# Expert stage of an attention and mixture-of-experts block: half-precision splitting in pairs of chunks, the second pair one tile later, and the routing weights applied on GpSimd

## What is computed

```python
a = xf @ W1a_e + b1a_e
b = xf @ W1b_e + b1b_e
y = jax.nn.silu(a) * b @ W2_e + b2_e
return (acc + w_e[:, None] * y, None)
```

## Time and profile before

| what | us |
|---|---|
| median of 3 runs | 671.4 (671.26 to 672.26) |
| span of the profiled execution, first to last instruction | 669.5 |
| from the first matmul of tile 2 to that of the last tile, 36 tiles | 160.99 |
| PE busy over the span | 575.0 |
| ACT busy, expert tiles 2 to 37 | 142.42 |
| DVE busy, the same tiles | 123.34 |

### The profile page before, as it was taken

One profiled execution on the slowest core, in us unless ns is written; L12 is line 12 of the kernel. 1 busy time (PEld: TensorE's weight loads), 2 busy tenths in 40 slices (PEclk: granted clock), 3 DMA queues, 4 the chain that ended last, 5 costly groups with the idle time before them and its releaser, 6 DMA issues.

```text
span 669.5 us, 19952 instructions
## 1 busy us (share of the span) xinstructions
PE 575.0 (86%) x5529; PEld 419.3 (63%) x5530; DVE 464.9 (69%) x1571; ACT 428.4 (64%) x1108; POOL 342.2 (51%) x501
## 2 busy tenths in 40 slices
PE   3599999999999999999999998218999999999700
PEld 1366666666666666666666665107888888888600
DVE  5665677787778768768767663454777777777646
ACT  3457665766767757766667655116888888888700
POOL 5432254565665655656656444650545545555553
PEclk9989999999999999999999999657999999999955
DMA  8212011112112112101212102132121211111066
GB/s 240 60 56 57 10 48 41 40 54 68 32 52 63 48 35 59 55 30 57 55 34 55 47 19 62 50 97 59 55 61 50 61 56 49 55 54 52 27 181 196
DMA packets 53668, 41.53 MB, mean 62 GB/s; under 512 B 7554, under 2 KB 48341, under 8 KB 53616
## 3 DMA queue, kind: packets, MB, share of 16 engines
q1 hardware_dynamic: 43056, 29.12, 16.4%
q0 software_dynamic: 4544, 8.54, 3.6%
q10 hardware_dynamic: 6016, 3.24, 1.6%
HBM read 24.80 MB, written 12.78 MB: 56 GB/s over the span
## 4 chain that ended last, share of the span: by engine, by line
PE 80%; DVE 7%; DMA 4%; issue 3%; ACT 2%; POOL 2%; SPq 0%; DVEq 0%; ACTq 0%; POOLq 0%
PE bank L1162 15%; PE bank L1126 8%; PE bank L1163 6%; PE bank L1319 5%; PE bank L1321 5%; PE bank L1320 5%; PE bank L1150 4%; PE bank L1139 4%; PE bank L1138 3%; PE bank L1340 3%; PE bank L1341 3%; PE bank L1114 3%; PE bank L1342 2%; PE bank L1175 2%; PE bank L1151 2%
## 5 line engine op out<-in xcount | busy, mean ns | idle before, releaser
L796 DVE TENSOR_REDUCE nmax<-bank 128x3 f32<-128x384 f32 x256 | 140.6, 555 | 75.5 <-PE bank L1126 71.1
L601 ACT ACTIVATE probs<-bank 128x384 f32<-128x384 f32 x256 | 126.7, 495 | 45.2 <-PE bank L1126 42.5
L1126 PE MATMUL bank<-cb,c 128*128 128x256 bf16 x512 | 140.6, 275 | 0.0
L554 POOL DMA_INDIRECT expert_outs<-y_sb,number_of x78 | 78.7, 1010 | 92.7 <-ACT y_sb L704 78.7
L1162 PE MATMUL bank<-probs,v_aug 128*32 128x256 f32 x512 | 119.1, 391 | 0.0
L1036 DVE SCALAR_TENSOR_TENSOR h<-bank,b_sb,silu_a 128x256 f32<-128x256 f32 x156 | 71.6, 479 | 51.4 <-ACT silu_a L715 51.2
L1319 PE MATMUL bank<-xt,we_hi 128*128 128x256 f16 x312 | 86.3, 277 | 1.9 <-ACT xt L689 0.8
L1320 PE MATMUL bank<-xt,we_hi 128*128 128x256 f16 x312 | 86.1, 276 | 0.0
L1321 PE MATMUL bank<-xt,we_lo 128*128 128x256 f16 x312 | 86.1, 276 | 0.0
L695 ACT ACTIVATE hh<-h 128x256 f16<-128x256 f32 x156 | 64.2, 411 | 19.1 <-DVE h L1036 14.4
L468 POOL DMA_INDIRECT expert_rows<-send,pos_i x64 | 63.3, 990 | 25.3 <-issue 12.2
(11 more groups left out here) (179 smaller groups left out, 1354.5 us busy)
## 6 DMA issues: line engine op xcount, KB each, us to landing
g_in<-expert_rows SPq DMA_DIRECT2D x39, 132.0 KB
k_pad<-qk_t SPq DMA_DIRECT2D x128, 32.0 KB, 1.9
mod_b<-mod_rows SPq DMA_DIRECT2D x16, 256.0 KB, 3.2
we_lo<-expert_outs SPq DMA_DIRECT2D x16, 256.0 KB, 3.9
wstage<-in_L_ffn_W1a_dram SPq DMA_DIRECT2D x16, 128.0 KB, 2.2
wstage<-in_L_ffn_W1b_dram SPq DMA_DIRECT2D x16, 128.0 KB, 2.3
wstage<-in_L_ffn_W_dram SPq DMA_DIRECT2D x16, 128.0 KB, 2.4
out_dram<-we_lo ACTq DMA_DIRECT2D x16, 128.0 KB, 3.5
```

Of the source, the lines that this page charges most:

```text
L554: pool.indirect_dma_start(out=outs, out_offset=bass.IndirectOffsetOnAxis(ap=number_of[:, r, s:s + 1], axis=0), in_=y_sb[:, r, s, :], in_of ...
L601: nc.scalar.activation(probs[:, k % 4], col_bank[k % 2][:, 0:S + P], ACT.Exp, scale=SM_SCALE).then_inc(probs_ready, 1)
L796: nc.vector.tensor_reduce(nmax[:, k], row_bank[k % 2][:, 0:3 * P].rearrange("p (c t) -> p c t", t=P), AX.X, ALU.max, negate=True).then_inc ...
L1126: return mm(diagonal, ident16, mask.unsqueeze(1).broadcast_to([P, 2, P]), start=False, stop=True, skip_group_check=True)
```

## The change

The copies `hh` and remainders `hl` are made for two chunks at once (512 columns) in place of one (256). The first pair (chunks 0 and 1) of tile j is made in tile j; the second pair (chunks 2 and 3) of tile j is made in tile j+1: on ACT behind the silu of chunk 0, on DVE behind h of chunk 1. `hl` counts two steps per tile in place of four. `weigh` leaves ACT: POOL multiplies by the weights (`tensor_scalar`, two instructions of 128 columns) ahead of its scatter. PE's list stays as it is.

```diff
@@ GpSimd, scatter(j) @@
-                pool.wait_ge(act_y, times(j, NS, NS))
+                pool.wait_ge(vec_y, times(j, 1, 1))
+                pool.wait_ge(named.sem, named.after(j, "weight"))
+                if due(times((j[0], 0, 1), 32)):
+                    pool.wait_ge(y_sent[r], times((j[0], 0, 1), 32))
                 pool.nop(nofuse=True)
                 for s in range(NS):
+                    nc.gpsimd.tensor_scalar(y_sb[:, r, s], yb[:, r % 2, s], weight_of[:, r, s:s + 1], 1.0, ALU.mult, ALU.mult).then_inc(pool_y, 1)
+                for s in range(NS):
+                    pool.wait_ge(pool_y, times(j, NS, s + 1))
+                    pool.nop(nofuse=True)
                     pool.indirect_dma_start(out=outs, ...
@@ ScalarE @@
-            def high(j, f):
-                act.wait_ge(vec_h, times(j, FB, f + 1))
+            def high(j, half):
+                two = slice(2 * half, 2 * half + 2)
+                act.wait_ge(vec_h, times(j, FB, 2 * half + 2))
                 if due(times(plus(j, -2), 1, 1)):
                     act.wait_ge(pe_y, times(plus(j, -2), 1, 1))
-                nc.scalar.activation(hh[:, j[1] % 2, f], h32[:, f], ACT.Copy).then_inc(act_hh, 1)
-
-            def weigh(j):
...
+                nc.scalar.activation(hh[:, j[1] % 2, two], h32[:, two], ACT.Copy).then_inc(act_hh, 1)
@@ ScalarE, tile(j), in the loop over f @@
-                    if f == 2 and finished:
-                        weigh(plus(j, -2))
+                    if f == 0 and following:
+                        high(plus(j, -1), 1)
                     if f == 2:
+                        high(j, 0)
                         read_next_experts(j)
-                    if f:
-                        high(j, f - 1)
-                high(j, FB - 1)
@@ VectorE @@
-            def low(j, f):
-                vec.wait_ge(act_hh, times(j, FB, f + 1))
-                nc.vector.tensor_tensor(hl[:, j[1] % 2, f], h32[:, f], hh[:, j[1] % 2, f], ALU.subtract).then_inc(vec_hl, 1)
+            def low(j, half):
+                two = slice(2 * half, 2 * half + 2)
+                vec.wait_ge(act_hh, times(j, 2, half + 1))
+                nc.vector.tensor_tensor(hl[:, j[1] % 2, two], h32[:, two], hh[:, j[1] % 2, two], ALU.subtract).then_inc(vec_hl, 1)
@@ VectorE, tile(j) @@
-                    if due(times(plus(j, -1), FB, f + 1)):
-                        vec.wait_ge(vec_hl, times(plus(j, -1), FB, f + 1))
+                    if due(times(plus(j, -1), 2, f // 2 + 1)):
+                        vec.wait_ge(vec_hl, times(plus(j, -1), 2, f // 2 + 1))
                     nc.vector.scalar_tensor_tensor(out=h32[:, f], ...
-                    if f >= 2:
-                        low(j, f - 2)
+                    if f == 1 and following:
+                        low(plus(j, -1), 1)
                     if f == 2:
                         read_next_experts(j)
-                low(j, FB - 2)
-                low(j, FB - 1)
+                low(j, 0)
@@ TensorE, project_out(j) @@
-                pe.wait_ge(vec_hl, times(j, FB, FB))
+                pe.wait_ge(vec_hl, times(j, 2, 2))
```

More of the change, by code:

```diff
@@ L269, in build @@
         pe_ab, act_silu, vec_h, act_hh, vec_hl = sem("pe_ab"), sem("act_silu"), sem("vec_h"), sem("act_hh"), sem("vec_hl")
-        pe_y, vec_y, act_y = sem("pe_y"), sem("vec_y"), sem("act_y")
+        pe_y, vec_y, pool_y = sem("pe_y"), sem("vec_y"), sem("pool_y")
         y_sent = [sem(f"y_sent{r}") for r in range(4)]
@@ L689, in save_x, with tile @@
                 nc.scalar.activation(xt[:, j[1] % 2], (chain_a16, chain_b16)[j[1] % 2][:, 0:2 * TS].rearrange("p (h t) -> p h t", t=TS), ACT.Copy).then_inc(act_x, 1)
-            def high(j, f):
-                act.wait_ge(vec_h, times(j, FB, f + 1))
+            def high(j, half):
+                two = slice(2 * half, 2 * half + 2)
+                act.wait_ge(vec_h, times(j, FB, 2 * half + 2))
                 if due(times(plus(j, -2), 1, 1)):
                     act.wait_ge(pe_y, times(plus(j, -2), 1, 1))
-                nc.scalar.activation(hh[:, j[1] % 2, f], h32[:, f], ACT.Copy).then_inc(act_hh, 1)
-            def weigh(j):
[L698 to L704, removed]
+                nc.scalar.activation(hh[:, j[1] % 2, two], h32[:, two], ACT.Copy).then_inc(act_hh, 1)
             known_experts, read_next_experts = experts_of(act)
-            def tile(j, more=True, finished=True):
+            def tile(j, more=True, following=True):
                 e = known_experts(j)[0]
@@ L717, in tile @@
                         save_x(plus(j, 1))
-                    if f == 2 and finished:
-                        weigh(plus(j, -2))
+                    if f == 0 and following:
+                        high(plus(j, -1), 1)
                     if f == 2:
+                        high(j, 0)
                         read_next_experts(j)
-                    if f:
-                        high(j, f - 1)
-                high(j, FB - 1)
             save_x(tile_number(0))
-            tile(tile_number(0), finished=False)
-            tile(tile_number(1), finished=False)
-            in_fours(act, 2, NT - 1, tile)
+            tile(tile_number(0), following=False)
+            in_fours(act, 1, NT - 1, tile)
             tile(tile_number(NT - 1), more=False)
-            weigh(tile_number(NT - 2))
-            weigh(tile_number(NT - 1))
+            high(tile_number(NT - 1), 1)
             out_v = out.rearrange("b (s p) d -> b p s d", p=P)
@@ L1019, in _, with tile @@
             vec.wait_ge(table, TABLE_STEPS)
-            def low(j, f):
-                vec.wait_ge(act_hh, times(j, FB, f + 1))
-                nc.vector.tensor_tensor(hl[:, j[1] % 2, f], h32[:, f], hh[:, j[1] % 2, f], ALU.subtract).then_inc(vec_hl, 1)
+            def low(j, half):
+                two = slice(2 * half, 2 * half + 2)
+                vec.wait_ge(act_hh, times(j, 2, half + 1))
+                nc.vector.tensor_tensor(hl[:, j[1] % 2, two], h32[:, two], hh[:, j[1] % 2, two], ALU.subtract).then_inc(vec_hl, 1)
             known_experts, read_next_experts = experts_of(vec)
-            def tile(j, finished=True):
+            def tile(j, finished=True, following=True):
                 e, last, before_last = known_experts(j)
@@ L1048, in bias_out @@
                 if due(times(plus(j, -2), NS, NS)):
-                    vec.wait_ge(act_y, times(plus(j, -2), NS, NS))
+                    vec.wait_ge(pool_y, times(plus(j, -2), NS, NS))
                 y = (o_bank, tail_bank)[j[1] % 2]
@@ L1052, in bias_out @@
                                         b2_sb[:, bass.ds(e, 1), :].broadcast_to([P, NS, D]), ALU.add).then_inc(vec_y, 1)
-            tile(tile_number(0), finished=False)
+            tile(tile_number(0), finished=False, following=False)
             tile(tile_number(1), finished=False)
@@ L1057, in _ @@
             e, last = tile(tile_number(NT - 1))
+            low(tile_number(NT - 1), 1)
             bias_out(tile_number(NT - 2), last)
```

## The result

| | median us | runs | ratio to before (95% interval) |
|---|---|---|---|
| before | 671.83 | 671.26 to 672.56, 4 runs | |
| after | 696.54 | 695.44 to 697.73, 4 runs | 1.0374 (1.0354 to 1.0395) |

The change costs 24.7 us. 695 was forecast, with a range of 685 to 705. The profiled execution has a span of 694.8 us, against 669.5.

A forecast was written before the change was run, and what follows sets the result against it. Before, PE in the expert stage was held by hl, behind a ring of ACT and DVE. 36 periods of 5.07 plus 1.4 give +22.9; +1.1 and -0.4 make +23.6 on 669.5, 693.1; median 1.9 above: 695 us, range 685 to 705.

The forecast's parts named there:

- The walk: Expert stage: chain from PE's hidden(j) through silu 1, h 1 and the remainder of j-1 to project_out; period 5.07 us.
- T0: Start of hidden(j) on PE, from which the forecast counts the times within a tile.
- The costs without a row: Instruction times estimated from similar rows: 512-column copy 0.62, 512-column remainder 0.68, POOL's tensor_scalar 0.45 us.
- The sum: 36 periods of 5.07 plus 1.4 for loop rounds, 183.9 against 160.99; with tile 1 and the end, +23.6 us.
- the rounds of the loop: Eight-tile rounds in the expert stage cost 0.7 us each; half kept over four rounds, 1.4 in all.
- Tile 1: Tile ahead of the 36 periods in the expert stage; claimed to get PE's new wait too, +1.1 us.
- The end: After the last hidden, POOL's last scatter is last: 13.6 us against 14.0 before, -0.4.
- PE at its floor: Rival: the chain fits under hidden(j), freeing ACT pays in full; 36 periods of 4.18, -10.5, 661 us; chance 0.05.
- The engines collide: Rival: POOL's weighing holds DVE's remainder on the chain; period up to 5.52, about 711 us; chance 0.08.
- No change: Rival: PE's wait is as long as the one before; period 4.47; chance 0.02.
- part of the wait: Rival: silu 1 and h 1 come early enough for a period of 4.6 to 4.8, 677 to 684 us; chance 0.05.
- The ring: ACT and DVE waiting for each other behind PE's wait for hl before the change; DVE's h 2 waited 0.56 us for silu.

The follow-up runs named there:

- e4_high_first: The changed kernel with ACT's pair copy of the tile before moved ahead of silu 0; 688.44 us, ratio 1.0266 to the kernel before.
- e5_split_wait: The changed kernel with PE's wait split: project_out starts on the first pair of remainders, waits for the second ahead of chunk 2; 673.13 us.
- e6_single_late: The changed kernel with chunks copied one by one again (256 columns), but in the change's order; 700.93 us, ratio 1.0458 to the kernel before.
- e3_weigh_act: The changed kernel with the weighing back on ACT, pairs and their order kept; 694.62 us, ratio 1.0363 to the kernel before.
- e8_more_pool: The changed kernel with one more tensor_scalar of 128 columns on POOL, ahead of its two; 696.97 us, ratio 1.0391 to the kernel before.
- e1_low_first: The changed kernel with DVE's pair remainder of the tile before moved ahead of h 0; 666.19 us, ratio 0.9950 to the kernel before.

## Why the prediction was right

**The walk.** Forecast 5.07 us a tile, measured 5.09, and link by link against the timelines above (start of the tile 542.83):

| link | forecast after T0 | measured |
|---|---|---|
| silu 0 | 0.96 | 543.78, 0.95 |
| pair copy of tile j-1 | 1.32 | 544.15, 1.32 |
| silu 1 | 1.84 | 544.67, 1.84 |
| h 1 | 2.45 | 545.28, 2.45 |
| remainder of tile j-1 | 2.84 | 545.68, 2.85 |
| project_out | 3.68 | 546.52, 3.69 |
| next hidden | 5.07 | 547.91, 5.08 |

Every link is a start or a duration of the earlier trace rows, so the mechanism was right and not only the number. e4_high_first, e5_split_wait and e6_single_late each change one link, and the period moved by close to what the walk gives for it (0.22, 0.65 and 0.17 a tile, for 0.22, 0.67 and 0.16).

**The costs without a row.** The groups of tile 2 to 38, after (mean ns behind the bar):

```profile
L703 ACT ACTIVATE hh<-h 128x512 f16<-128x512 f32 x72 | 45.3, 630 | 0.0
...
L1019 DVE TENSOR_TENSOR hl<-h,hh 128x512 f16<-128x512 f32 x73 | 49.8, 682 | 0.0
...
L557 POOL TENSOR_SCALAR y_sb<-yb,weight_of 128x128 f32<-128x128 f32 x72 | 26.0, 367 | 43.4 <-DVE yb L1046 43.4
```

The pair copy was taken at 0.62 and took 0.630, the pair remainder at 0.68 and took 0.682. POOL's `tensor_scalar` was taken at 0.45 and takes 0.367: too dear, and without effect.

**The sum.** The 36 periods were put at 183.9 and took 185.67: the rounds of the loop were taken to keep half of their 0.7 us, they keep 0.6 (41.33 less eight times 5.09). With 5.09 in place of 5.07 that is the whole: 36 times 5.09 and four times 0.6 make 185.7. Tile 1 was put at +1.1 and gave little. Its wait is there, 1.08 us at 463.89, but from the first hidden to tile 2 the kernel took 9.82 after and this before:

```profile
454.97:464.48 9.51, 9.51 (x80) 7.86 (x81) 4.42 (x11) 6.04 (x16) 0.60 (x4) 0.73 0.29 67
```

The granted clock over that stretch is 0.84 after and 0.73 before (third number from the right): PE went from 1.2 to 2.4 GHz 3.1 us after the first hidden instead of 5.1. PE's busy time in the stretch is 0.77 shorter for it (8.74 and 9.51), which gives back most of the wait. What moved the rise was not tested. The end was put at 13.6 us from the last hidden to POOL's last scatter and took 13.6 (14.0 before). The two misses, +1.8 and -0.8, partly cancel. Of the 25.3 by which the spans differ (23.6 forecast), another 0.5 lies ahead of the first hidden matmul, where the change touches nothing.

**The rivals.** *PE at its floor* failed by its own condition: the links from the end of chunk 1 to project_out take 2.2, not 1.37. The rule of the Trainium skill behind it ("VectorE: DVE Perf Modes", The TRN2 errata) is borne out in what it says: one instruction of 512 columns took 0.682 where two of 256 take 0.75, and e6_single_late shows 0.17 us a tile for copies and remainders together. It says nothing of what such an instruction waits for. *The engines collide*: in the changed kernel the weighing (543.84 to 544.56) is over long before the remainder on the chain (545.68), as the walk had it, and e3_weigh_act and e8_more_pool show no share in the time. What does meet POOL is the other remainder, which is off the chain (last section). *No change* and *part of the wait* did not come.

**What was said to look for.** PE waits on `hl` in every tile, 26.8 us in all (some 30 said); ACT is idle 2.0 us a tile (over 1.5 said). POOL's y_sb rows take 0.37 and not 0.45. The ring, in which h waits for a silu, was to be gone as a cause: h still waits for a silu in every tile (0.38 at 545.28), now as a link of PE's own chain.

## What to carry to other kernels

When work is put off to a later tile, ask what stands ahead of it there on its engine, and follow that back: if it leads to the very engine that waits for the deferred work, the wait is in every iteration, and freeing another engine did not help here (694.6 us with the weighing on ACT, 696.5 on POOL). Move the deferred piece to the front of the iteration, where it depends only on the iteration before (666 us with the remainder moved, 661 with the copy moved as well, against 697). Test the halves of a change apart: here one half alone (the weights on POOL, 659.5 us, ratio 0.984) beats both kernels, and the other hid it.

## What the runs showed of the hardware

In these traces a pair remainder on DVE (two inputs in SBUF) and one of POOL's copies or weighings (which read SBUF) exclude each other, and the later one waits for the earlier to end. The timeline of POOL in the changed kernel, beside the DVE rows at 542.30 and 545.68 above:

```profile
542.38 0.65 POOL L544 COPY number_of<-g_in 128x2 int32<-128x2 int32 x1
542.97 0.18 POOL L545 COPY weight_of<-g_in 128x2 f32<-128x2 f32 x1
543.84 0.72 POOL L557 TENSOR_SCALAR y_sb<-yb,weight_of 128x128 f32<-128x128 f32 x2 [0.69 <-DVE yb L1046]
545.02 1.06 POOL L561 DMA_INDIRECT expert_outs<-y_sb,number_of  x1 [0.47 <-POOL y_sb L557]
546.39 0.97 POOL L561 DMA_INDIRECT expert_outs<-y_sb,number_of  x1 [0.30 <-issue]
```

The copy at 542.38, two columns wide, took 0.65 us where the same instruction takes 0.21 in the kernel before: it ends at 543.03, just behind DVE's remainder (542.30 to 542.98). In the 36 periods twelve of these copies start up to 0.17 after a remainder did, and every one of them ends 0.04 after it. The weighing at 543.84 meets no remainder and takes 0.72 for two. The scatter at 545.02 does overlap one (545.68 to 546.36), but takes no longer for it: the first scatter of a tile takes 1.06 in e1_low_first too where it meets none. In e1_low_first it goes both ways. The timelines of DVE and POOL there:

```profile
543.82 0.85 DVE L1019 TENSOR_TENSOR hl<-h,hh 128x512 f16<-128x512 f32 x1 [0.68 <-ACT hh L703]
```

```profile
543.76 0.21 POOL L545 COPY weight_of<-g_in 128x2 f32<-128x2 f32 x1
543.91 1.26 POOL L557 TENSOR_SCALAR y_sb<-yb,weight_of 128x128 f32<-128x128 f32 x2
```

POOL's small copy (543.76 to 543.97) was there first: the remainder took 0.85 in place of 0.68. The weighing that started during the remainder took 1.26 for two in place of 0.72. With the rule quoted in the prediction (the Trainium skill, "SBUF — State Buffer", Who interferes with whom) the trace agrees, in both orders. A collision costs time only where the instruction that is held up is one that PE waits for: in the changed kernel none is, and in e1_low_first five are, at 0.05 to 0.15 us each.
